# A cross-attention block and a top-2 expert layer in one program: the experts' first tiles begun beside the last block's router

## The reference

```python
x = x + xattn(layernorm(x), ctx, Wq, bq, Wk, bk, Wv, bv, Wo, bo)      # 16 heads of 32
h = layernorm(x)
w = softmax(h @ W_router.T + b_router)                                # 8 experts
w = w, kept at each token's two largest and zero elsewhere
x = x + sum over experts e of w[e] * (h @ W_experts[e].T + b_experts[e])
```

## Time and profile before

| | us |
|---|---|
| median of 3 executions | 1407.37 |
| lowest, highest | 1406.43, 1410.46 |
| the profiled execution, its own time | 1413.48 |
| its span, first to last instruction | 1411.8 |
| mean granted clock of PE | 0.935 |

### The profile page before, as it was taken

The page is one execution under the profiler, slowest core; times in us unless marked ns, Lnnn a source line. Parts: engine busy times, 40 slices in busy tenths (PEclk is TensorE's granted clock), DMA queues, the critical chain, the costliest instruction groups (busy, mean ns, idle before and its releaser), DMA issues. The chain is left out here.

```text
span 1411.8 us, 37249 instructions
## 1 busy us (share of the span) xinstructions
PE 1244.1 (88%) x11616; PEld 746.8 (53%) x11617; DVE 856.4 (61%) x1891; ACT 635.4 (45%) x914; POOL 791.6 (56%) x1034
## 2 busy tenths in 40 slices
PE   6596899999899899899899997722899999999997
PEld 3253666656556556566566665411445555555554
DVE  3363787878578678678677766441444544544544
ACT  2114467645645645654654574200333434434433
POOL 3103347677567577667667766662265545544554
PEclk9787799999899999999999998765999999999999
DMA  6624437565555555645645556654689988989986
GB/s 230 190 60 130 129 95 217 139 208 172 147 198 166 166 180 170 197 154 189 184 127 182 179 158 248 224 214 160 120 168 177 173 167 169 180 168 173 171 171 123
DMA packets 135727, 239.05 MB, mean 169 GB/s; under 512 B 18240, under 2 KB 49216, under 8 KB 134464
## 3 DMA queue, kind: packets, MB, share of 16 engines
q1 hardware_dynamic: 101952, 156.99, 36.8%
q0 software_dynamic: 29824, 67.27, 24.2%
q10 hardware_dynamic: 3840, 13.20, 2.5%
HBM read 112.84 MB, written 101.22 MB: 152 GB/s over the span
## 5 line engine op out<-in xcount | busy, mean ns | idle before, releaser
L1794 PE MATMUL Yp<-we_s,gT_hi 128*128 x1088 | 347.9, 381 | 6.4 <-DVE gT_lo L1742 5.7
L1701 POOL DMA_INDIRECT out<-yw,to x136 | 211.1, 1552 | 235.0 <-issue 95.3
L1061 POOL TENSOR_TENSOR we_s<-P_s,we_s 128x1024 f16<-128x1024 f32 x112 | 237.4, 2131 | 75.0 <-ACT we_s L854 58.3
L1794 PE MATMUL Yp<-we_s,gT_lo 128*128 x544 | 207.2, 381 | 0.0
L1718 ACT ACTIVATE gT_hi<-Tp 128x512 f16<-128x512 f32 x138 | 82.3, 596 | 276.0 <-PE Tp L1781 274.2
L1760 DVE SCALAR_TENSOR_TENSOR yb<-Yp,be_s 128x512 f32<-128x512 f32 x136 | 94.1, 692 | 167.6 <-PE Yp L1794 162.5
L903 DVE TENSOR_REDUCE mx_sb<-S 128x6 f32<-128x924 f32 x160 | 171.9, 1114 | 20.5 <-PE S L660 16.2
L643 PE MATMUL W<-we_s,wq_s 128*128 128x512 f16 x512 | 161.5, 393 | 14.1 <-DVE we_s L891 6.0
L1794 PEld LDWEIGHTS Yp<-we_s,gT_hi 128*128 128x128 f16 x1088 | 106.9, 98 | 121.7 <-issue 10.4
L681 PE MATMUL W<-wo_s,aT_hi 128*128 128x512 f16 x512 | 167.9, 390 | 0.0
L1140 POOL DMA_INDIRECT dispatched<-xn,idx x128 | 127.5, 996 | 49.9 <-issue 30.8
(11 more groups left out here) (188 smaller groups left out, 2133.3 us busy)
## 6 DMA issues: line engine op xcount, KB each, us to landing
xg<-dispatched SPq DMA_DIRECT2D x140, 257.0 KB
we_s<-we_s SPq DMA_DIRECT2D x192, 128.0 KB, 2.6
be_s<-in_x SPq DMA_DIRECT2D x16, 1024.0 KB, 6.0
xR_s<-in_x SPq DMA_DIRECT2D x16, 1024.0 KB, 9.4
out<-xR_s SPq DMA_DIRECT2D x16, 1024.0 KB
wst<-in_weT SPq DMA_DIRECT2D x16, 512.0 KB
we_scratch<-wsp SPq DMA_DIRECT2D x16, 512.0 KB, 4.0
we_s<-we_scratch ACTq DMA_DIRECT2D x8, 1024.0 KB, 7.8
```

The source lines that it names most:

```text
L1061: e.tensor_tensor(Pst[1][:, r:r + 2, :], exps(n), Pst[0][:, r:r + 2, :], ALU.subtract).then_inc(pldp, 1)
L1701: e.indirect_dma_start(out, bass.IndirectOffsetOnAxis(ap=to[u][:, :], axis=0), yw[u % YW][:, :], None, bounds_check=N - 1, oob_is_err=Fals ...
L1794: m = e.matmul(Yp[:, u % 2, :], gT[u % 2][xp][:, k, :], we_s[:, bass.ds(n * WN + (wp * KC + k) * D, D)], start=(c == 0), stop=(c == 11))
```

## The change

The experts' tiles become part of the first program. Their buffers lie over attention buffers (`xg` over `P32_s`, `gT` over `wq_s`, `yb` over `att`, `yw` over `xn1`, `Tp` over `PVp`, `Yp` over two banks of `S`); the meeting of all engines goes. After the `dve_RE` of block 13, DVE works out a table of the first 104 tiles (TILEA), the whole tiles of the first 14 blocks, by expert: by counts of 13, 13, 11, 13, 15, 16, 10 and 13. The remaining 32 tiles are tabled after the last block: 2, 5, 2, 4, 3, 4, 2 and 5 by expert, then 5 spare. A table has a tile per partition (24 and 22 operations on 128 x 8 or less) and is brought to one partition by a DMA. The steps of the last block's router are taken out of the slots and put between tiles.

```diff
+    NTB = (24, 22)
+    def table_counts(e, part):      # 7 operations, a sync after each
...
+    def table_experts(e, part, ch): # 8 (part 0) or 6 operations
...
+    def table_rows(e, part, ch):
...
+        ch.do(e.tensor_scalar(tcol[part][:, 0:1], te[:, 5:6], float(SPARE // P), float(P), ALU.min, ALU.mult))
+        ch.do(e.tensor_scalar(tcol[part][:, 1:2], te[:, 0:1], float(NE - 1), None, ALU.min))
+        ch.do(e.tensor_scalar(tcol[part][:, 2:3], te[:, 2:3], tile_p[:, 0:1], 16.0, ALU.is_equal, ALU.mult))
+    def load_table(e, part):
+        first, n = (TILEA, MAXT + AHEAD - TILEA) if part else (0, TILEA)
+        e.wait_ge(tbd, sum(NTB[:part + 1]))
+        e.dma_start(tbl[0:1, 3 * first:3 * (first + n)], tcol[part][0:n, :]).then_inc(ld_t[part], 16)
 def dve_RE(e, b):
...
+        if b.reg is None and b.c == EARLY - 1:
+            ch = table_counts(e, 0)
+            table_experts(e, 0, ch)
+            table_rows(e, 0, ch)
 def act_ATh(e, b, i):
...
             act_load_experts(e, 3, 5)
+            load_table(e, 0)
+        if b.last and i == 3:
+            act_load_experts(e, 5, NE)
 # in the slots: R, RX, RB, RM, RS, RE, RI, SC of bm2 and SD, XS of bm3, each
-        if on_bm2:
+        if on_bm2 and not bm2.last:
...
+    def of_tile(e, i, c, most):
+        return e.value_load(tbl[0:1, bass.ds(i * 3 + c, 1)], min_val=0, max_val=most)
 SP, after the slots
-            (wait zset, zero rows, wait ld_ew, st_x1, all scatters; end of the block; loads)
+            e.wait_ge(phd, 10 * NB)
+            e.wait_ge(pldp, NP * NB)
             for p in range(2):
                 for k in range(TOPK):
+                    e.wait_ge(scat[p][k], 64 * EARLY // 2)
+            e.wait_ge(ld_t[0], 16)
+            for u in range(XG): sp_load(e, 0, u)
+            sp_XS(e, LAST)
+            for u in range(XG): sp_load(e, 0, XG + u)
+            sp_zero_rows(e)
+            for u in range(XG): sp_load(e, 1, u)
+            load_table(e, 1)
+            turns(e, lambda it: sp_turn(e, it), 1, TURNA - 1, lambda: sp_rest_stored(e))
 POOL, after the slots (whose last step is now SD of block 14) and the two memsets
+            pool_SC(e, LAST)
+            pool_add(e, 0, 0)
+            pool_add(e, 0, 1)
+            pool_SD(e, LAST)
+            for u in range(2, TU): pool_add(e, 0, u)
+            turns(e, lambda it: pool_turn(e, it), 1, TURNA, lambda: e.wait_ge(ld_t[1], 16))
 ACT, after the slots
-            act_load_experts(e, 5, NE)
+            act_hi(e, 0, 0); act_hi(e, 0, 1); act_hi(e, 0, 2)
+            act_weigh(e, 0, 0)
+            act_RX(e, LAST)
+            (hi(u + 2), weigh(u) for u = 1 to 7; then the turns)
 DVE, after the slots
-            tables(e)
+            (waits for ld_ew, ld_t[0])
+            dve_glo(e, 0, 0); dve_glo(e, 0, 1)
+            dve_RB(e, LAST); dve_RM(e, LAST)
+            dve_tile(e, 0, 0)
+            dve_RS(e, LAST); dve_RE(e, LAST)
+            dve_tile(e, 0, 1)
+            dve_RI(e, LAST)
+            dve_tile(e, 0, 2)
+            (table_counts(1), tile 3, table_experts(1), tile 4, table_rows(1), tiles 5 to 7, turns)
 PE, after the slots
+            (waits for ld_t[0], ld_ew)
+            pe_turn_rows(e, 0, 0); pe_turn_rows(e, 0, 1)
+            pe_tile(e, 0, 0)
+            pe_tile(e, 0, 1)
+            pe_R(e, LAST, Blk(NB - 1 - (-2)))
+            for u in range(2, TU): pe_tile(e, 0, u)
+            turns(e, lambda it: pe_turn(e, it), 1, TURNA, lambda: e.wait_ge(ld_t[1], 16))
```

More of the change, by code:

```diff
@@ L1531, in pool_slot @@
             pool_PL(e, b, 9)
-        if on_bm3:
+        if on_bm3 and not bm3.last:
             pool_SD(e, bm3)
@@ L1564, in slots, with done, added, tile @@
             slot(e, Blk(s))
+    BASE = 8
+    LAST = Blk(NB - 1)
+    def done(i):
+        return i + 1 + BASE
+    def added(it, u):
+        return it * (16 * TU // YW) + 16 * (u // YW + 1)
+    def tile(it, u):
+        return it * TU + u
+    def in_loop(it):
+        return not isinstance(it, int)
+    def of_tile(e, i, c, most):
+        return e.value_load(tbl[0:1, bass.ds(i * 3 + c, 1)], min_val=0, max_val=most)
+    def turns(e, turn, first, split, waits):
+        with e.Fori(first, split) as it:
+            turn(it)
+        waits()
+        with e.Fori(split, NTURN) as it:
+            turn(it)
@@ new lines, in sp_rest_stored, with pool_add @@
+    def sp_rest_stored(e):
+        e.wait_ge(ld_t[1], 16)
+        e.wait_ge(zst, 16 * (NE + 1))
+        for p in range(2):
+            e.wait_ge(st_x1[p], 16 * NB // 2)
+            for k in range(TOPK):
+                e.wait_ge(scat[p][k], 64 * NB // 2)
+    def pool_add(e, it, u):
+        i = tile(it, u)
+        e.wait_ge(ywd, done(i))
+        e.wait_ge(wtd, done(i))
+        hold(e)
+        if in_loop(it) or u >= 2 * YW - 1:
+            new = of_tile(e, i, 2, 16)
+            for back in range(1, YW):
+                e.wait_ge(add_y[(u - back) % YW], added(it, u - back) - 16 + new)
+            hold(e)
+        elif u > 0:
+            e.wait_ge(add_y[(u - 1) % YW], added(it, u - 1))
+        e.indirect_dma_start(out, bass.IndirectOffsetOnAxis(ap=to[u][:, :], axis=0), yw[u % YW], None,
+                             bounds_check=N - 1, oob_is_err=False, compute_op=ALU.add).then_inc(add_y[u % YW], 16)
@@ new lines, in pe_tile @@
+    def pe_tile(e, it, u):
+        i = tile(it, u)
+        n = of_tile(e, i, 1, NE - 1)
+        e.wait_ge(gl, done(i))
+        e.wait_ge(ye, done(i - 2))
+        seqs = [q for k in range(KC) for q in split3(k)]
+        for c, (xp, wp, k) in enumerate(seqs):
+            m = e.matmul(Yp[:, u % 2, :], gT[u % 2][xp][:, k, :], we_s[:, bass.ds(n * WN + (wp * KC + k) * D, D)],
+                         start=(c == 0), stop=(c == 11))
+        m.then_inc(yp, 1)
+        pe_turn_rows(e, it, u + 2)
```

418 lines of the change are left out of this document (211 added, 207 removed).

## The result

The changed kernel takes 0.9941 of the time of before, interval 0.9926 to 0.9957, medians 1404.13 and 1413.22 us over 20 executions of each: some 8 us faster (6 to 10 by the interval), where 18 were forecast. (The 20 executions of before have a median 5.9 us above the three shown ahead of the prediction, so only differences on the same chips are used from here on.) The profiled execution has a span of 1401.0 us against 1411.8, 10.8 less; the profiles are of single executions, and T0 alone varied between 936.8 and 946.6 among eleven that run the same work up to it.

What follows compares the result with a forecast made beforehand. Two clocks set the end: T0 + 3.03 us a tile, and serial adds from about tile 7 to 13. Terms -36.8 + 16.8 + 2.0 = -18.0 us from the median 1407.4 gave 1389.4 us, range 1374 to 1402 (8 in 10).

Steps and rivals of the forecast that it cites:

- T0: Start of the first tile's transposes on PE; forecast at 941.6 us, 36.8 us earlier than before.
- The first table on DVE: Table operations behind `base` of block 13: 3.7 us, of which 2.0 remain on PE and DVE, bounds 0 and 3.7.
- the weights' loads: Loads of experts 5 to 7 before the first tiles: end at 935, cost 0, hidden by the wait for scatters.
- POOL's queue: Scatters and memsets ahead of add 0, more between adds 1 and 2: add 6 and PE 16.8 us later against T0.
- clock and loops: Lower granted clock after tiles with gaps, and the second loop's start: 2 us together, bounds 0 and 5.
- SP's queue: Zero-row stores of 9.5 us ahead of tile 8's load, out at T0 + 28.5: cost 0 beside the adds, otherwise 7 us.
- The last 32 tiles: Eight new experts' adds, each 5.8 us behind the one before: cost 0, bound 6 us if an add takes 7 us.
- The first: Rival for the first tiles: serial adds don't hold PE, gain towards 36.8 us, 1370 us; chance 0.12 for below 1380.
- the fourth: Rival at the seam: the early start doesn't happen, T0 near the old one, time within 4 us of before; chance 0.04.
- The second: Rival at the seam and first tiles: T0 or adds come later, 4 us gain at worst, 1397 to 1403; chance 0.20.
- The third: Rival, slower: scatters and zero stores stretch the serial adds; gain gone at 8.3 us a cycle; chance 0.08.
- The second loop: Start of the loop over the last tiles: shared a 2 us term with the clock, bounds 0 and 5.

Runs made afterwards that it cites:

- open_adds: The changed kernel without the rule that adds 1 to 6 each wait for the one before; ratio 0.9899 to the kernel before.
- late_apart: The changed kernel with the adds of the last 32 tiles sent to four scratch tensors, without new-expert waits; ratio 0.9884 to the kernel before.
- mid_waits: The changed kernel with eight more full waits of adds, in turns 5 to 8 (tiles 40 to 71); ratio 1.0043 to the kernel before.

## Why the prediction was right and wrong

**T0.** The time came out right, 941.6 forecast and 940.8 found, but partly by luck. From `base` of block 13 to T0 the forecast had 941.6 - 883.3 = 58.3 us, and it took 61.3; this execution made up for it by reaching `base` 3.6 us earlier. Whether the changed kernel gets there earlier as a rule isn't settled: its eleven profiles have 875.5 to 884.3, the two of before 883.1 and 885.7. Two terms were off, in opposite directions. *The first table on DVE* was mis-sized: "I take 2.0, bounds 0 (all hidden) and 3.7 (nothing hidden)". From `base` to the next `xR_s` DVE takes 7.96 us (7.85 to 7.96 in all eleven), and the last scatter of block 13 comes 6.7 us later against `base` than before (54.35 and 47.66). But for two of the 24 operations the 3.7 us would have been nearly right: L1078 and L1082 take 2.09 and 2.10 us, where others of 128 x 8 take 0.17; with 0.17 for these two it would be 4.1 us. Each has two inputs, and begins and ends within 0.07 us of one of POOL's 128 x 1024 operations (L1120, at 881.11 and 883.47, 2.13 and 2.12 us long); in the ten other kernels too the long ones end with an operation of POOL. That DVE waits for POOL there is a reading of these times, and no run tries it apart. The table did push the row numbers of block 13, as written: POOL waited 6.12 us for them. In the other direction, from the end of the last scatter to T0 it took 6.0 us and not 7.9. The early start ended on the scatters of block 13, as written, and the weights' loads set nothing.

**POOL's queue.** Right in mechanism and nearly in size. Add 0 at T0 + 24.0 (24.3), SD of block 15 between adds 1 and 2: 7.81 us apart (7.7). Adds 1 and 3 stood 7.15 and 7.34 us behind the ones before, where I had 5.7 to 5.8, beside scatters and zero stores; in the three other profiles with the same order there, add 1 has 5.7 to 5.8 and add 3 6.4 to 7.9, so this varies from execution to execution. Add 6 came 18.5 us later against T0 (16.8). Held up to tile 25: 20.0 us more, against 16.8 + 2.0 for clock and loops. The granted clock over 960 to 980 was 0.75. SP's queue, "Cost 0 beside the adds", was later than I had it: the load of tile 8 went out at T0 + 32.5 and not 28.5, for the zero stores took 11.17 us and not 8.02, and tile 8's transposes at T0 + 37.9 ended a wait of 5.03 us for it. I had tile 8 held until T0 + 37 by the adds anyway, so it cost little here; `open_adds` shows it alone. From the Trainium skill's 2.0 us plus bytes (DMA: Bandwidth & Descriptors, Anatomy of one DMA) I had estimated an add cycle of 4.5 us; the trace disagrees, for none of the steps between the serial adds 1 to 6, in any kernel here, is below 5.39.

**The last 32 tiles.** This step failed: "Cost 0 by that; bound 6 us, if an add takes 7 us there". It cost 6.8 us, more than the bound, although the adds were 6.5 us in the mean and not 7. The eight new experts' adds stood 5.9, 5.0, 6.5, 6.1, 7.3, 6.9, 7.1 and 7.2 us behind those before, 6.5 in the mean instead of 5.8. I had taken 5.8 from one wait for waits that follow a burst. With 6.5 the sum reads 8 x 3.5 = 28 us lost against 28 made up, and a balance over the whole hides that the lag is at its largest before the end: add 126 (1374.69) came 76.8 us after add 104 (1297.89), 10 us more than 22 tiles take, which four `yw` with 6 us of cover don't hide. PE pays for it at tiles 127, 129, 134 and 135, the last with 4.4 us. That these waits are the cause is shown: without them (`late_apart`) nothing is held, and eight more of them elsewhere (`mid_waits`) hold PE there.

**Sum.** -33.9 + 20.0 + 6.8 = -7.1 us against -36.8 + 18.8 + 0 = -18.0: of the 10.9 us missing, 6.8 are the last 32 tiles, 2.9 lie before T0 and 1.2 in the first 25 tiles. The medians say 8, within 6 to 10. The profiles' 10.8 has besides the 3.6 us by which the changed one was ahead at `base`.

**The rivals.** The first (adds don't hold PE) is refuted by the kernel of before with adds not serial and by the 20.0 us more held here, the fourth by T0. The second has the outcome in its size and part of the cause: the table pushed block 13's last scatter further than its "full table", but the landing wasn't late, most cycles weren't 7 us, and most of the loss lay in the last 32 tiles, which it doesn't name. The third's mechanism was there, at 5.5 to 7.8 us a cycle instead of 8.3 (and six steps, not seven, lie between adds 0 and 6). **The second loop** costs nothing: tiles 104 to 112, its first turn, run at 3.03 us each; the stall that the Trainium skill gives for a taken branch whose target isn't in the fetched pages (Runtime: NRT & Kernel Launch, Instruction fetch mechanics) shows in no row here. Whether these loops' targets lie outside those pages isn't known, so this doesn't speak against the page.

## What to carry to other kernels

Work pulled forward into an idle stretch brings its own queue: before counting the idle time as gain, lay out what the in-order engines and the DMA engines must still do there, and place it one piece at a time between the pieces that the bound engine waits for (here, with the first adds' serial rule gone and the zero stores moved too, 27 of 29 us, of which the moved stores took 4.5 back). A small operation's price read in a quiet stretch needn't hold beside another engine's long ones: two operations of 24 account for 3.9 of the table's 7.96 us. And before a start time is called right, take it from the last point that the change doesn't touch. A wait whose price was read where it stood alone must not be charged at that price where it recurs every few steps, and its cover must be checked as a running lag, not as a balance at the end. What isn't read until later (zero rows, second-choice scatters) should not be stored first, but it isn't free later either.

## What the runs showed of the hardware

- Behind an accumulating indirect DMA of 128 rows of 2 KB the next one that had to wait for its landing followed after 5.5 to 6.6 us in 73 of 77 cases where the adds had come about 3 us apart, and after 7.1 to 8.0 us in all 15 cases behind a burst 1.86 us apart. Beside scatters and zero stores it was 5.7 to 7.9 us.
- Eight stores of 257 KB, issued from SP one behind the other, took 8.0 us at a DMA share of 0.61 (two kernels), 11.2 to 12.1 us at shares of 0.91 to 1.04 (five kernels) and 16.12 us at 1.03 (`open_adds`): where the DMA engines are full the queue that issues is slower too, but the share alone doesn't say by how much.
- Two DVE operations on 128 x 8 took 2.0 to 2.1 us instead of 0.17 in all eleven kernels with the table; each time they ended within 0.03 us of an operation of POOL on 128 x 1024.
- T0 varied by almost 10 us (936.8 to 946.6) among the eleven profiled executions of kernels that do the same work up to it. Up to `base` of block 13 they already differ by 8.8 us (875.5 to 884.3), so most of the variation lies in the attention part.
